# First batch projected before its scaling, and the row maxima transposed by a float32r product

## The reference

```python
def _layernorm(x): return (x - mean) / sqrt(var + 1e-5)        # no weights
q = _layernorm(x) @ Wq + bq ;  k = ctx @ Wk + bk ;  v = ctx @ Wv + bv
a = softmax(q k^T / sqrt(32)) v                                # per head
x = x + tanh(g_xattn) * (a @ Wo + bo)
x_q, x_scale = int8 rows of _layernorm(x), scaled by their largest magnitude
x = x + tanh(g_ffn) * ((x_q @ weight_q^T) * x_scale * weight_scale + bias)
```

## Time and profile before

| | us |
|---|---|
| median of 3 executions | 842.94 (842.88 to 843.11) |
| the profiled execution | 844.04 |
| its span, first to last instruction | 842.2 |
| PE busy | 822.0 |
| DVE / ACT / POOL busy | 533.7 / 512.9 / 507.2 |

### The profile page before, as it was taken

How to read it: one execution, slowest core, us unless ns; L and a number is a source line. 1 busy time by engine, 2 the same in 40 slices (tenths; PEclk the granted TensorE clock), 3 DMA queues, 4 the chain that set the end, 5 groups by cost and what they waited for, 6 DMA issues and landing times.

```text
span 842.2 us, 16102 instructions
## 1 busy us (share of the span) xinstructions
PE 822.0 (98%) x6340; PEld 517.5 (61%) x6340; DVE 533.7 (63%) x758; ACT 512.9 (61%) x712; POOL 507.2 (60%) x514
## 2 busy tenths in 40 slices
PE   7999999999999999999999999999999999999996
PEld 6755566656666656666656656656656656656553
DVE  5764558666567666658566576666658655566568
ACT  3565566665665656566565665666666665665675
POOL 3525475574767647495574767647485574665587
PEclk9999999999999999999999999999999999999999
DMA  8512604233241421314222241422314122111112
GB/s 320 170 54 98 194 26 138 77 85 109 64 138 52 147 77 46 126 51 155 77 78 98 56 163 51 136 67 69 125 51 138 63 54 86 39 51 51 51 51 100
DMA packets 39578, 79.62 MB, mean 95 GB/s; under 512 B 6864, under 2 KB 8272, under 8 KB 37456
## 3 DMA queue, kind: packets, MB, share of 16 engines
q1 hardware_dynamic: 38928, 77.75, 29.2%
q10 hardware_dynamic: 576, 0.85, 0.3%
HBM read 61.78 MB, written 16.81 MB: 93 GB/s over the span
## 4 chain that ended last, share of the span: by engine, by line
PE 67%; DVE 16%; POOL 6%; issue 6%; ACT 3%; DMA 2%; SPq 0%; DVEq 0%; POOLq 0%; ACTq 0%
PE bank_b L322 21%; PE bank_a L322 11%; PE scores L361 7%; PE pv_ps L390 6%; PE sum_ps L392 6%; PE scores L376 5%; DVE row_max L1038 5%; DVE xt_lo L1028 3%; PE bank_a L436 3%; POOL x L1349 2%; DVE u_sb L1118 2%; PE bank_a L344 2%; DMA x_in<-in_x 2%; POOL x L1362 2%; POOL o_lo L1353 2%
## 5 line engine op out<-in xcount | busy, mean ns | idle before, releaser
L1038 DVE TENSOR_REDUCE row_max<-scores 128x16 f32<-128x1920 f32 x64 | 138.2, 2159 | 124.8 <-PE scores L361 124.8
L1362 POOL TENSOR_TENSOR x<-x,u_sb 128x512 f32<-128x512 f32 x56 | 75.7, 1352 | 159.3 <-DVE u_sb L1118 157.1
L735 ACT ACTIVATE probs<-scores 120x2048 f32<-120x2048 f32 x64 | 120.4, 1881 | 64.6 <-PE scores L380 64.3
L1353 POOL TENSOR_TENSOR o_lo<-on,o_hi 128x512 fp32r<-128x512 f32 x63 | 86.7, 1377 | 74.8 <-ACT o_hi L751 74.1
L1028 DVE TENSOR_TENSOR xt_lo<-xt,xt_hi 128x512 fp32r<-128x512 f32 x64 | 65.4, 1042 | 65.1 <-ACT xt_hi L698 65.0
L1357 POOL TENSOR_TENSOR x<-x,gbias_r 128x512 f32<-128x512 f32 x64 | 82.1, 1284 | 37.5 <-ACT cen L757 36.5
L361 PEld LDWEIGHTS scores<-k_sb,q_sb 32*128 32x128 f32 x2048 | 63.2, 186 | 52.2 <-issue 51.3
L1319 POOL TENSOR_TENSOR xt<-xt,rstd_b 128x512 f32<-128x512 f32 x60 | 91.9, 1556 | 2.7 <-ACT rstd_b L972 1.6
L1349 POOL TENSOR_TENSOR x<-x,gbo_r 128x512 f32<-128x512 f32 x64 | 88.4, 1391 | 3.2 <-DMA x<-in_x 3.1
L751 ACT ACTIVATE o_hi<-on 128x512 fp32r<-128x512 f32 x64 | 40.4, 631 | 73.0 <-DVE on L1051 72.9
L376 PE MATMUL scores<-q_sb,k_sb 32*120 32x512 f32 x512 | 72.6, 636 | 3.5 <-DVE row_max L1038 2.8
(11 more groups left out here) (176 smaller groups left out, 1788.4 us busy)
## 6 DMA issues: line engine op xcount, KB each, us to landing
xt<-in_x_t SPq DMA_DIRECT2D x16, 1024.0 KB, 5.4
x<-in_x SPq DMA_DIRECT2D x64, 256.0 KB, 3.0
out_x<-x SPq DMA_DIRECT2D x61, 256.0 KB, 2.3
x_in<-in_x SPq DMA_DIRECT2D x60, 256.0 KB, 4.0
rstd_b<-rstd_rows SPq DMA_DIRECT2D x14, 256.0 KB, 4.5
ctx_sb<-in_ctx_t SPq DMA_DIRECT2D x8, 360.0 KB, 5.2
probs<-in_wq SPq DMA_DIRECT2D x1, 1024.0 KB, 5.7
x<-in_wo SPq DMA_DIRECT2D x1, 1024.0 KB, 11.8
```

Source lines behind the costliest of these rows:

```text
L735: act.activation(probs[0:KEYS], scores[0:KEYS], ACT.Exp, scale=SCALE).then_inc(p_ready, 1)
L1038: dve.tensor_reduce(row_max[:].rearrange("p (t r) j -> p r t j", r=ROWG)[:, :, :, j], scores[:, :, 0:QT * KEYS].rearrange("p r (t k) -> p ...
L1353: pool.tensor_tensor(o_lo[i % 2][:, j], on[:, j % 2], o_hi[i % 2][:, j].bitcast(F32), ALU.subtract).then_inc(o_split, 1)
L1362: pool.tensor_tensor(x1_of(m)[:, t], x1_of(m)[:, t], u_sb[:], ALU.add).then_inc(out_ready, 1)
```

## The change

Five things. (1) Wq is loaded in four parts with a semaphore each, and PE begins the column means with the first; `keep_running` is 5 instead of 14 products. (2) In batch 0 the transposed x is not scaled. The query tile 0 is projected in fp32 straight from the centred Wq and x (`project_q_whole`), the three others in three passes of unscaled parts, and the queries are multiplied by the inverse deviations afterwards (`scale_q0` on DVE out of PSUM, then `bias_q0` on ACT in place). (3) The loads are reordered: second half of Wk and the transposed x ahead of the four x tiles that only the statistics need; the statistics follow the centring on DVE, and `x_rstds(0)` follows the low part of Wq on POOL. (4) `spread_rstd(0)` stands in the middle of query tile 1, `spread_rstd(1)` behind the first value passes; `high_max(0)` and `copy_max(0)` each stand one `high_x` earlier. (5) `turn_max` is, for all batches, four float32r products with a float32r identity in place of four fp32 transposes. `x_scaled` no longer counts batch 0, so the counts waited for are one batch lower and the waits the same.

The diff, with the unchanged surroundings cut:

```diff
-ident_f = sb("ident_f", [P, P])
+ident_r = sb("ident_r", [P, P], F32R)
...
 bk_landed, wk_landed = sem("bk_landed"), [sem(f"wk_landed{h}") for h in range(2)]
-bq_landed, wq_landed = sem("bq_landed"), sem("wq_landed")
+bq_landed, wq_landed = sem("bq_landed"), [sem(f"wq_landed{c}") for c in range(DT)]
...
 rstd_stored, rstd_landed = sem("rstd_stored"), sem("rstd_landed")
-rstd_spread, rstd_copied = sem("rstd_spread"), sem("rstd_copied")
+rstd_spread, rstd0_copied, rstd_copied = sem("rstd_spread"), sem("rstd0_copied"), sem("rstd_copied")
+ident_ready, q0_scaled = sem("ident_ready"), sem("q0_scaled")
...
 wq_stage, wv_stage, wo_stage = probs, x1[1][:, 0:CT], x1[0]
-mean_of = inv_sum[:, 0:P]
+mean_of, rstd0, ident_stage = inv_sum[:, 0:P], inv_sum, rstd_b[:, 0:P]
...
             sp.wait_ge(x_split, nth(n - 1, DT, 3))
+        if n == 1:
+            sp.wait_ge(q_done, nth(0, DT, 0))
...
         sp.wait_ge(rstd_stored, 16 * (n - 1))
-        sp.wait_ge(x_scaled, nth(n - 1, DT, 3))
+        sp.wait_ge(x_scaled, nth(n - 2, DT, 3))
...
-    load(wq_landed, wq_stage[:], rows(wq))
+    for c in range(DT):
+        load(wq_landed[c], wq_stage[:, c], rows(wq)[:, c])
...
     load(wk_landed[0], wk_sb[:, :, 0:D // 2], rows(wk)[:, :, 0:D // 2])
+    load(wk_landed[1], wk_sb[:, :, D // 2:D], rows(wk)[:, :, D // 2:D])
+    load_xt(0)
...
         load(x0_landed[t], x0_stage[t], x_v[0, t])
-    load(wk_landed[1], wk_sb[:, :, D // 2:D], rows(wk)[:, :, D // 2:D])
-    load_xt(0)
...
         for c in chunks:
-            if j == 0:
+            if j == (n == 0):
...
                 ins.then_inc(q_done, 1)
+
+    def project_q_whole(j, bank):
+        pe.wait_ge(xt_landed, 16)
+        for c in range(DT):
+            pe.wait_ge(wq_centred, c + 1)
+            ins = pe.matmul(bank[:], wq_stage[:, c, j * P:(j + 1) * P], xt[:, c], start=c == 0, stop=c == DT - 1)
+        ins.then_inc(q_done, 1)
...
         for t in range(QT):
-            ins = pe.transpose(bank[:, t * P:(t + 1) * P],
-                               max_sp[:, t * ROWG:(t + 1) * ROWG].rearrange("p r c -> p (r c)").bitcast(F32),
-                               ident_f[:])
+            ins = pe.matmul(bank[:, t * P:(t + 1) * P], max_sp[:, t * ROWG:(t + 1) * ROWG].rearrange("p r c -> p (r c)"),
+                            ident_r[:], start=True, stop=True)
...
         if n > 0:
-            pe.wait_ge(x_scaled, nth(n - 1, DT, 3))
+            pe.wait_ge(rstd0_copied, 1)
         for t in range(QT):
-            ins = pe.transpose(sum_ps[:, t * P:(t + 1) * P], ln_rstd[:, t:t + 1].broadcast_to([P, P]), ident_f[:])
+            ins = pe.transpose(sum_ps[:, t * P:(t + 1) * P], ln_rstd[:, t:t + 1].broadcast_to([P, P]), ident_r[:].bitcast(F32))
...
     pe.wait_ge(consts_ready, 5)
-    keep_running(14, pv_ps)
-    pe.wait_ge(wq_landed, 16)
+    keep_running(5, pv_ps)
     for c in range(DT):
+        pe.wait_ge(wq_landed[c], 16)
...
         pe.wait_ge(wk_landed[j // 2], 16)
-        if j == 2:
-            pe.wait_ge(ident_landed, 16)
-            spread_rstd(0)
         project_k(0, j, scores[:, j])
-    for c in range(DT - 1):
-        project_q(0, 0, bank_a, [c])
-        project_q(0, 1, bank_b, [c])
-    project_q(0, 0, bank_a, [DT - 1])
-    project_q(0, 1, bank_b, [DT - 1])
+    project_q_whole(0, bank_a)
+    project_q(0, 1, bank_b, first)
+    pe.wait_ge(ident_ready, 1)
+    spread_rstd(0)
+    project_q(0, 1, bank_b, second)
...
     scores_by_query(0, 0)
-    project_q(0, 2, bank_a, first)
-    spread_rstd(1)
+    project_q(0, 2, bank_a)
...
     scores_by_query(0, 1)
-    project_q(0, 2, bank_a, second)
-    project_q(0, 3, bank_b, first)
+    project_q(0, 3, bank_b)
...
     scores_by_query(0, 2)
-    project_q(0, 3, bank_b, second)
     pe.wait_ge(wv_lo_done, CT)
-    project_v(0, bank_a, range(1))
+    project_v(0, bank_a, range(2))
+    spread_rstd(1)
...
     scores_by_query(0, 3)
-    project_v(0, bank_a, range(1, CT))
+    project_v(0, bank_a, range(2, CT))
...
     def high_x(n, c):
-        act.wait_ge(x_scaled, nth(n, DT, c))
         if n > 0:
+            act.wait_ge(x_scaled, nth(n - 1, DT, c))
             act.wait_ge(q_done, nth(n - 1, DT, 3))
+        else:
+            act.wait_ge(xt_landed, 16)
...
         act.activation(q_sb[:, j], bank[:], ACT.Identity, bias=bq_c[:, j:j + 1]).then_inc(q_ready, 1)
+
+    def bias_q0(j):
+        act.wait_ge(q0_scaled, j + 1)
+        act.activation(q_sb[:, j], q_sb[:, j], ACT.Identity, bias=bq_c[:, j:j + 1]).then_inc(q_ready, 1)
...
-    load(ident_landed, ident_f[:], consts_f32)
+    load(ident_landed, ident_stage, consts_f32)
     act.preload_act_table_set("natural_log_exp_and_others")
+    act.wait_ge(ident_landed, 16)
+    act.activation(ident_r[:], ident_stage, ACT.Copy).then_inc(ident_ready, 1)
...
         high_wq(c)
+    for c in range(DT):
+        high_x(0, c)
...
         bias_k(0, c, scores[:, c])
-        high_x(0, c)
     high_ctx(0)
+    act.wait_ge(rstd_spread, 1)
+    act.activation(rstd0[:], sum_ps[:], ACT.Copy).then_inc(rstd0_copied, 1)
+    act.wait_ge(bq_landed, 16)
+    bias_q0(0)
...
     act.activation(pick[:], picks[:], ACT.Copy, scale=-1.0).then_inc(pick_ready, 1)
-    act.wait_ge(bq_landed, 16)
-    bias_q(0, 0, bank_a)
     act.wait_ge(wv_landed, 16)
-    for c in range(CT):
+    act.activation(wv_hi[:, 0], wv_stage[:, 0], ACT.Copy).then_inc(wv_hi_done, 1)
+    bias_q0(1)
+    for c in range(1, CT):
         act.activation(wv_hi[:, c], wv_stage[:, c], ACT.Copy).then_inc(wv_hi_done, 1)
-    bias_q(0, 1, bank_b)
...
     act.preload_act_table_set("natural_log_exp_and_others")
-    bias_q(0, 2, bank_a)
+    bias_q0(2)
+    bias_q0(3)
...
                    ACT.Copy).then_inc(rstd_copied, 1)
-    bias_q(0, 3, bank_b)
...
     copy_v(0, bank_a)
+    high_max(0)
     high_x(1, 1)
-    high_max(0)
+    copy_max(0, pv_ps)
     high_x(1, 2)
-    copy_max(0, pv_ps)
+    copy_v(1, bank_b)
     high_x(1, 3)
-    copy_v(1, bank_b)
...
-    def scale_x0(c):
-        dve.wait_ge(rstd_spread, 1)
-        dve.wait_ge(xt_landed, 16)
-        dve.tensor_tensor(xt[:, c], xt[:, c], sum_ps[:], ALU.mult).then_inc(x_scaled, 1)
+    def scale_q0(j, bank):
+        dve.wait_ge(rstd0_copied, 1)
+        dve.wait_ge(q_done, nth(0, DT, j))
+        dve.tensor_tensor(q_sb[:, j], bank[:], rstd0[:], ALU.mult).then_inc(q0_scaled, 1)
...
     dve.memset(magic[:], MAGIC).then_inc(consts_ready, 1)
+    for c in range(DT):
+        centre_wq(c)
...
     for c in range(DT):
-        centre_wq(c)
-    scale_x0(0)
-    scale_x0(1)
-    low_x(0, 0)
-    scale_x0(2)
-    low_x(0, 1)
-    scale_x0(3)
-    low_x(0, 2)
-    low_x(0, 3)
+        low_x(0, c)
+    x_statistics(1, 0)
+    scale_q0(0, bank_a)
+    x_statistics(1, 1)
+    scale_q0(1, bank_b)
     low_ctx(0)
-    for t in range(QT):
-        x_statistics(1, t)
     maxima(0, 0)
+    x_statistics(1, 2)
+    scale_q0(2, bank_a)
     maxima(0, 1)
+    x_statistics(1, 3)
+    scale_q0(3, bank_b)
...
     pool.wait_ge(consts_ready, 1)
-    x_rstds(0)
...
         pool.tensor_tensor(wq_lo[:, c], wq_stage[:, c], wq_hi[:, c].bitcast(F32), ALU.subtract).then_inc(wq_lo_done, 1)
-    x_rstds(1)
+    x_rstds(0)
...
         pool.tensor_tensor(wv_lo[:, c], wv_stage[:, c], wv_hi[:, c].bitcast(F32), ALU.subtract).then_inc(wv_lo_done, 1)
+    x_rstds(1)
```

## The result

The changed kernel takes 840.64 us in the median of 18 runs (839.85 to 842.61), the one before 842.96 (842.57 to 844.76, 18 runs): a ratio of 0.9973, with a 95% interval of 0.9966 to 0.9979. The profiled execution took 840.9 us, against 844.04 before.

A forecast was written before the change was run, and what follows sets the result against it. PE was taken as the bound: away from the ends, a us of PE is a us of time. 844.04 - 2.8 (prologue) + 0.1 (turn) = 841.3 us profiled; median 1.10 lower, 840.2, range 837.6 to 844.4.

The forecast's parts named there:

- Term 1: Prologue: step 0 begins sooner, taken as 2.8 us gained, own range 0.4 to 4.3.
- The means: Prologue, PE: column means start near 4.4 us with Wq's first part and end at 9.6, against 11.4 before.
- Centring, Wq, keys, fp32 tile: Prologue: centring from 9.8 us, POOL's low parts of Wq 11.2, keys 9.6, whole fp32 query tile 14.5 to 17.9.
- The low parts: Prologue: low parts of x meet POOL's last subtraction; first two done at 17.7 us, the others by 19.9.
- The two new links: Prologue: copy of the spread row and query scaling lie on the path, costing 1.3 us of the gain.
- The port: Before step 0: DVE's `low_max` and batch 1's low parts meet POOL's scalings; gain 2.5 down to 0.4 if held to POOL's end.
- the milder one: DVE let in between two POOL instructions: `low_max` ends about 37.7 us, step 0's scores at 39.2, batch 1's projection held 0.7.
- Term 2: Turn of the maxima, 16 times: weight loads limit each product to 0.11 us; taken as 0, +0.1 in all.
- rival A: Turns run at the fp32 rate, +0.42 us each, +6.8 in all: 846.9 us; chance 0.17, a third of it half way.
- C: Turns gain as columns do, -3.4 us over sixteen turns: 836.8 us; chance 0.07.
- Rival D: Prologue: filler's removal does nothing, means end as before, only statistics order counts: about 841.5 us; chance 0.18 together with another rival.

The follow-up runs named there:

- e12: Kernel before with only the three new orders of e10 and nothing of the change: 840.90 us.
- e1: Changed kernel with the turn of the maxima as before, by four fp32 transposes: 840.46 us.
- e2: Changed kernel with the turn of the maxima as four plain fp32 products: 841.79 us.
- e3: Changed kernel with ACT copying the turned maxima before the high part of x chunk 2, not after: 840.30 us.
- e5: Changed kernel with DVE's dequantisation of tile 1 moved between the two last low parts of x, instead of behind both: 839.73 us.
- e6: Changed kernel with the new orders of both e3 and e5: 838.34 us.
- e10: Kernel of e6 with ACT also adding the keys' bias before rounding the high parts, in steps that make keys: 838.12 us.
- e11: Kernel of e10 with the turn of the maxima in plain fp32 products: 845.86 us.
- e4: Changed kernel with 14 filler products instead of 5: 841.78 us.
- e8: Kernel before with early means alone (Wq in four loads, 5 fillers, centring before statistics, deviations later), x still scaled before projection: 845.54 us.
- e9: Kernel of e8 with PE kept busy by filler products while it waits for the inverse deviations: 847.68 us.

## Why the prediction was right, step by step

The forecast was 840.2 in a range of 837.6 to 844.4; the median is 840.64. The sign, the two terms and the place of the gain held.

**Term 1, 2.8 us.** Measured 3.1 in the span, 2.3 in the medians; both are inside its own range. The sum from 844.04 gave 841.3 for a profiled execution, which took 840.9; the 1.10 us between execution and median that I took over from before was only 0.3 here, so the two errors partly cancel. I had treated that 1.10 as a constant of profiling. By e12 it is in all likelihood the long hold of a low part by POOL (1.13 us at step 0's scores), which I had in the path that the change shortens, and took off once more with the 1.10. Without that the median's forecast is 841.3, so that 0.4 us between forecast and median, in place of 0.7, are in part luck.

- *The means.* Forecast to run from 4.4 to 9.6, four records at 0.85 us and four at 0.43. They ran from 3.97 to 9.29, as told. The clock's rise was taken as fixed near 7.6 us; it varies. The means ended at 8.77, 7.93, 8.36, 9.01, 8.75 in other kernels with this very start (e1, e2, e3, e5, e6), and in none of the five were they the last: the second chain, from the landing of x through the statistics, was longer there, by up to 1 us (e2). The forecast had that chain, but not that it was as long.
- *Centring, Wq, keys, fp32 tile.* 9.8, 11.2, 9.6 and 14.5 forecast for their starts; 9.33, 10.83, 9.13 and 13.99 measured. Right, shifted by the means' start.
- *The low parts.* The step in which I had a collision with POOL that isn't there: first two by 17.7 and the others by 19.9, measured 18.85 for all four. The statistics ended at 16.47 (15.6 forecast) and so came after POOL's Wq. The hold fell on POOL's deviation operations instead, and cost nothing.
- *The two new links* were on the path: last pass, copy, scaling, bias, scores at 21.69 for 22.2.
- *The port.* For `low_max` neither outcome was put to the test: it took 0.25 us at 37.12 (37.4), and POOL's second scaling ended at 37.28. For batch 1's low parts the milder one came: the first two took 2.03 and 2.02 us (from 37.29 and 39.24), each through the one scaling that POOL had begun (37.25 to 38.78, 38.73 to 40.71), the four 5.18. Step 0's scores at 38.92 for 39.2. The low parts give back 0.43 us by L400, for the 0.7 of the forecast. The page SBUF — State Buffer of the Trainium skill, section Who interferes with whom, has a hold for the whole of the other's instruction. Here the trace agrees, and so does the 1.84 us of e12, while the 3.10 us of rows 5, in the same place, showed a hold through two.

**Term 2, the turn: 0.** Right, by the price that I took: the four products start 0.11 us apart, the pitch of their weight loads, so columns in one pass saved nothing (first to next line 0.40, 0.44 before). That the load is what sets the 0.11 was argued from rows 10; no run has a product without a load of its own. The page TensorE: Matmul & The Clock Gate, section LDWEIGHTS, of the Trainium skill gives a load's time as its columns over 1.2 GHz, which makes an estimate of 0.107 us for 128. The 0.11 of the trace agrees. But the step before it was wrong, the one from a busy share of 98% to the sentence that away from the ends a us of PE is a us of time; e2 shows that it was not. At +0.49 us a turn, beyond the full form of rival A (+0.42), the time rose by 1.2 us and not by 7.8. Rival A's price of 6.8 us and its break-even of +0.17 us a turn rested on that sentence, and so did C's gain: e12 against e10 loses 0.026 us a step for the 0.04 of its turn, and e1 against the changed kernel nothing that the medians show. The chances of A and C were right to be small, their prices were too large by far. The 7.7 us of e11 don't restore the sentence, since half of what its steps lose is a wait of its own. The 0 for the term was right because the turn itself cost the same, not because the steps are full.

**Rival D** had the filler's removal do nothing: with 14 fillers (e4) 1.1 us of the gain of 2.3 go, about half is left, so neither it nor its opposite holds. The means alone (e8) gain nothing either: the passes wait for the deviations until 19.5, and the clock is lost meanwhile. So the early means need the first tile, which needs no deviations and fills PE from 14 to 17 us. How the rest divides between that tile, the new order of the loads and the scaling of the queries is open: no run has one of them without the others.

## What to carry to other kernels

A matmul engine that is 49.83 of 50 us busy can still have slack: its modelled ends cover short waits. Read start to start at the joints of a step, beside the busy time, and prove the slack by adding work (here +0.49 us a turn: 1.2 us of 7.8). Then look at what else the added work moves: with three orders changed the same turn cost 7.7 us, of which half was a wait that the new orders had tied to it. A wait of 0.1 to 0.6 us that is removed alone came back at the next joint in e3, and half of it in e5, so move the orders of two engines together. An idle stretch ahead of matmuls can cost twice, by itself and by the clock behind it (e8): fill it with useful products, as the fp32 tile does, before buying an earlier start elsewhere. And compare a second profile of the same stretch before explaining a us of it: 1.1 us of the gain at step 0 was a hold that one execution of before had and e12 had not.

## What the runs showed of the hardware that I had not expected

- Waits of PE of 1.7 to 2.5 us stood ahead of every fall of the granted clock that I saw: to 0.57 at 19.5 us in e8, to 0.58 at 79 us in e9. In the profiled execution of e6 it fell after a wait of 1.7 us for a row maximum near 744 us, and the last step took 1.7 us more; that of e12 lost as much in the same place. Window of e6:

```profile
746.00:750.00 4.00, 4.00 (x20) 2.65 (x13) 1.61 (x4) 3.83 (x5) 1.28 (x1) 0.63 0.03 12
```

  e10 has the same wait (PE busy 2.26 of 4 us from 742 to 746, 2.25 in e6) and kept its clock at 1.00, and in the profile of before the passes behind the wait of 2.40 us stand 0.23 us apart, the higher level. So a wait of that length can, but need not, cost it. The executions of e12 lie at 840.6 to 840.9 or at 842.3 to 842.7, and the profile with the fall is one of the latter; that the fall is what parts them is likely, not shown.
- At the start the profile's granted clock reads 1.00 while the records are those of the lower level: eight means of 3.60 us or 6.68, by when the rise came.
- A float32r product over 128 columns costs 0.11 us from start to start, an fp32 transpose 0.11, a plain fp32 product 0.22 in two records.
- One and the same instruction, a low part of x on DVE against POOL's subtractions, took 3.10 us in the profile of before and 1.84 in that of e12, with starts that differ by 0.06 us: held through two of POOL's instructions or through one.
